# Column sums of the pruned attention gathered in 32 partitions of one column group instead of 4 x 8 rows in four

## The reference, cut to what matters

```
scores = softmax(einsum('bhqd,bhkd->bhqk', q, k) / sqrt(8))   # B=8, H=16, 128 x 128
col_sum = sum(scores, axis=2)                                 # over the queries: (B, H, 128)
_, idx = top_k(col_sum, int(128 * 0.9))                       # keeps 115, drops 13
mask = 1 at idx, 0 elsewhere
out = einsum('bhqk,bhkd->bhqd', scores * mask[:, :, None, :], v)
```

## Time and profile before

| | |
|---|---|
| median of 3 runs | 852.5 us (851.77 to 853.15) |
| the profiled execution's own time | 851.77 us |
| its span in the trace | 850.1 us |
| PE busy over the span | 730.0 us (86%) |
| mean granted clock of PE | 0.911 of full |
| pruned attention, first scores to last output | about 546.6 to 616.3 us |

### The profile page before, as it was taken

One profiled execution on the slowest core, in us unless ns is written; L12 is line 12 of the kernel. 1 busy time (PEld: TensorE's weight loads), 2 busy tenths in 40 slices (PEclk: granted clock), 3 DMA queues, 4 the chain that ended last, 5 costly groups with the idle time before them and its releaser, 6 DMA issues. The chain is left out here.

```text
span 850.1 us, 14512 instructions
## 1 busy us (share of the span) xinstructions
PE 730.0 (86%) x4910; PEld 610.7 (72%) x4910; DVE 557.7 (66%) x1478; ACT 415.5 (49%) x1279; POOL 374.2 (44%) x375
## 2 busy tenths in 40 slices
PE   5984899998999999986559999699769999994755
PEld 3653699997899998875557888466558888883754
DVE  6897664346799989874546677668645566655535
ACT  3891343443455555442135777389424466652221
POOL 6753212203566643533123776556431488872001
PEclk9798799999899999997879999869869999997678
DMA  7000010110000000000003444000100323100000
GB/s 268 2 1 25 13 50 27 49 49 1 1 1 2 7 2 1 2 1 0 7 19 128 138 134 156 2 1 3 38 26 10 108 84 111 52 12 0 1 1 25
DMA packets 14276, 33.11 MB, mean 39 GB/s; under 512 B 1744, under 2 KB 5864, under 8 KB 13952
## 3 DMA queue, kind: packets, MB, share of 16 engines
q1 hardware_dynamic: 14208, 32.26, 11.3%
HBM read 31.63 MB, written 0.62 MB: 38 GB/s over the span
## 5 line engine op out<-in xcount | busy, mean ns | idle before, releaser
L1205 PE MATMUL banks<-input_hi,weights_in_lo 128*128 128x512 f32 x296 | 125.9, 426 | 27.0 <-PEq L1482 14.1
L1205 PE MATMUL banks<-input_lo,weights_in_hi 128*128 128x512 f32 x296 | 120.9, 408 | 0.0
L1205 PE MATMUL banks<-input_hi,weights_in_hi 128*128 128x512 f32 x296 | 120.2, 406 | 0.0
L1205 PEld LDWEIGHTS banks<-weights_out,hidden 128*128 128x128 f32 x864 | 100.5, 192 | 3.1 <-DVE hidden L2232 1.0
L1205 PE MATMUL banks<-weights_out,hidden 128*128 128x128 f32 x864 | 101.3, 275 | 0.7 <-ACT att_feat L1124 0.7
L985 ACT ACTIVATE probabilities<-banks,neg_max 128x128 f32<-128x128 f32 x256 | 90.7, 425 | 14.2 <-DVE neg_max L1877 14.1
L1071 ACT ACTIVATE hidden<-banks,cols 128x512 f32<-128x512 f32 x80 | 54.2, 688 | 78.9 <-ACTq L1069 78.9
L697 POOL TENSOR_TENSOR rstd<-var_eps,neg_half 128x4 f32<-128x4 f32 x24 | 25.1, 1044 | 151.5 <-POOLq L696 139.9
L1205 PEld LDWEIGHTS banks<-input_hi,weights_in_lo 128*128 128x128 f32 x296 | 58.8, 199 | 41.3 <-issue 29.4
L807 POOL TENSOR_TENSOR hidden<-hidden,scratch 128x512 f32<-128x512 f32 x48 | 62.1, 1293 | 19.2 <-ACT hidden L1090 16.7
L1205 PEld LDWEIGHTS banks<-input_hi,weights_in_hi 128*128 128x128 f32 x296 | 58.8, 198 | 13.5
(11 more groups left out here) (272 smaller groups left out, 1759.9 us busy)
## 6 DMA issues: line engine op xcount, KB each, us to landing
scratch<-cw_rows SPq DMA_DIRECT2D x19, 512.0 KB, 3.8
weights_out<-w_in SPq DMA_DIRECT2D x17, 256.0 KB, 2.7
weights_in<-w_in SPq DMA_DIRECT2D x8, 512.0 KB, 3.6
weights_in<-w_in SPq DMA_DIRECT2D x9, 256.0 KB, 3.0
weights_in<-w_in SPq DMA_DIRECT2D x16, 128.0 KB, 2.2
weights_out<-w_in SPq DMA_DIRECT2D x16, 128.0 KB, 2.2
wq<-w1q_in SPq DMA_DIRECT2D x1, 1024.0 KB, 4.9
wo<-w1o_in SPq DMA_DIRECT2D x1, 1024.0 KB, 7.0
```

What stands on the lines that cost most here:

```text
L1205: return pe.matmul(o, l, rh, start=start, stop=stop, **kw)
```

## The change

The eight one-column windows of a unit become eight 32-column blocks of their own, 128 x 32 each, with the inverse sum of head i in column 8 * (n % 4) + i of block i. All eight matmuls of a unit now write the same 32 partitions (0 to 31), where row 8 * (n % 4) + i is head i of unit n. What follows works on 32 partitions: ranking, mask, and the transpose of the mask (moving operand 32 columns of the identity instead of 128, output 128 x 32 instead of 128 x 128). `keep_values` reads the turned mask as 32 adjacent columns. `r_spread` keeps its size and place.

```
-        r_spread = scratch[:, 8:10, :].rearrange("p a t -> p (a t)")
+        r_spread = scratch[:, 8:10, :].rearrange("p a (u h m) -> p (a u) h m", h=8, m=2 * H)
-        ranked = sb("ranked", [P, P + 8])
-        top = sb("top", [P, 2, 8])
-        kept = sb("kept", [P, P])
+        ranked = sb("ranked", [2 * H, P + 8])
+        top = sb("top", [2 * H, 2, 8])
+        kept = sb("kept", [2 * H, P])
         def own_inverse(n):
-            at = 7 + 256 * (n % 4)
-            return r_spread[:, at:at + 7 * 32 + 1:32]
-
-        def inverse_column(n, i):
-            at = 7 + 256 * (n % 4) + 32 * i - (2 * (n % 4) + i // 4)
-            return r_spread[:, at:at + 32]
+            flat = r_spread[:, n % 4, :, :].rearrange("p h m -> p (h m)")
+            at = 8 * (n % 4)
+            return flat[:, at:at + 7 * (2 * H + 1) + 1:2 * H + 1]
                     for i in range(8):
-                        own = slice(32 * (i % 4), 32 * (i % 4) + 32)
-                        m = mm(bank[4 + n // 4 % 2][own, 0:P], inverse_column(n, i),
+                        m = mm(bank[4 + n // 4 % 2][0:2 * H, 0:P], r_spread[:, n % 4, i, :],
                                prob[:, n // 2 % 2, 8 * (n % 2) + i, :],
-                               start=(n % 4 == 0 and i < 4), stop=(n % 4 == 3 and i >= 4))
+                               start=(n % 4 == 0 and i == 0), stop=(n % 4 == 3 and i == 7))
-                    pe.transpose(bank[4 + n // 4 % 2][:, P:2 * P], kept[:, :], ident[:, :])\
+                    pe.transpose(bank[4 + n // 4 % 2][:, P:P + 2 * H], kept[:, :], ident[0:2 * H, 0:2 * H])\
-                    dve.tensor_scalar(ranked[:, 0:P], sums[:, P - 1::-1][:, 0:P], -1.0, None,
+                    dve.tensor_scalar(ranked[:, 0:P], sums[0:2 * H, P - 1::-1][:, 0:P], -1.0, None,
-                    kept_at = bank[4 + n // 4 % 2][:, P:2 * P].rearrange("p (j m) -> p m j", j=4)[:, 0:8, :]
-                    four = "p b (g j) c -> p (b g) j c"
+                    kept_at = bank[4 + n // 4 % 2][:, P:P + 2 * H]
-                    dve.tensor_tensor(v_kept[:, :, :, :].rearrange(four, j=4), v_wide[:, :, :, :].rearrange(four, j=4),
-                                      kept_at[:, :, :, None].broadcast_to([P, 8, 4, 32]),
+                    dve.tensor_tensor(v_kept[:, :, :, :].rearrange("p b h c -> p (b h) c"),
+                                      v_wide[:, :, :, :].rearrange("p b h c -> p (b h) c"),
+                                      kept_at[:, :, None].broadcast_to([P, 2 * H, 32]),
                                       ALU.mult).then_inc(v_kept_ready, 1)
```

## The result

The changed kernel takes 867.14 us (median of 4 runs, 865.85 to 867.96), the kernel before beside it 852.65 (851.77 to 853.15): a ratio of 1.0170, with a 95% interval of 1.0152 to 1.0187. It is slower by 14.5 us; 867.5 was forecast, with a range of 862 to 891. The profiled execution has a span of 864.2 us against 850.1.

What follows compares the result with a forecast made beforehand. PE was taken to bound the stage's half-clock stretch and ACT the full-clock one, with PE the bound after the change. The profiled 851.8 us, +15.8 for longer sums and -0.1 for the other edits gave 867.5, range 862 to 891.

Steps and rivals of the forecast that it cites:

- The price of a group: Column sums: sixteen instructions queue in group 0 at 107 ns, 1.86 us for 0.58; +1.28 us a unit, +2.56 at half clock.
- Both bounds: Column sums, each unit: +0 if narrow weights alone are fast (chance 0.03), +3.0 us if weight loads no longer hide (0.04).
- The estimate from the page: Column sums: four groups gain 3.2 rather than 4, so a unit loses 1.17 us, the stage some 1.5 us less.
- The change of the bound: Plain step at full clock: PE takes 3.78 us, over ACT's 3.31, so PE becomes the bound and ACT waits.
- two variants: Whole stage: two half-clock steps end the last sums at 624.2, +17.5 us; one ends them at 620.9, +14.2.
- the middle: Whole stage: +15.8 us, taken between +17.5 for two half-clock steps and +14.2 for one.
- the cases in which sums in one group don't bring the clock back or let it fall: PE clock: low until first kept values, +36 us, 888, chance 0.24; falling after each batch, some +50, 902, chance 0.12.
- The sentence that weighed these cases: Against the clock falling after kept values: full-clock rows show 2.0 us of wide work in 3.3 and no fall.
- The edits at nothing: Mask transpose, ranking on 32 partitions, `keep_values`, strided inverse sums: all told -0.1 to -0.8 us, taken as -0.1.
- up to 2 us either way: Chain after the last sums: where exactly the clock falls again is worth up to 2 us, slower or faster.

Runs made afterwards that it cites:

- the first experiment: The changed kernel with matmul i of a unit writing group i % 4 again, ranking, mask and its transpose still on 32 partitions: 851.09 us, ratio to before 0.9994.
- the second experiment: The kernel before with only all eight matmuls of a unit writing group 0, ranking on 128 partitions and wide mask transpose kept: 865.47 us, ratio 1.0172.
- the last experiment: The changed kernel with 14 identity transposes before its first scores and 12 before the scores of unit 2: 863.77 us, ratio to the kernel before 1.0175.

## Why the prediction was right

**The price of a group.** Forecast +1.28 us a unit at full clock and +2.56 at half; measured 1.87 - 0.58 = 1.29 and 3.55 - 1.01 = 2.54. It came from two unlike rows: 64 instructions that go round four groups, and eight transposes in one. Both bounds fall, +0 (which would have needed 0.65 us for the sixteen) and +3.0. One argument was circular, though: the 107 ns "that a transpose needs" is four times the 27 and stands in no row, where transposes take 99 or 128 ns.

The estimate from the page "TensorE: Matmul & The Clock Gate" of the Trainium skill, Part 3, which gives 2.38 times for three column groups at 512 columns a matmul (here 128), was +1.17, less than the 1.29 measured. But it was taken on 1.71 us, without the 0.15 of entry and exit. Of the whole row four groups give 1.87 / 0.58 = 3.2 times and three 1.87 / 0.78 = 2.4, which is what the page and the estimate from it say; 3.2 times of 1.87 us is a loss of 1.29 as well. The full factor of four is in the pitch alone (107 ns against 27), so the prediction set aside a figure that these runs agree with.

**The change of the bound.** Forecast a plain step of 3.78 bound by PE; measured 3.79, with PE at 14.00 of 14.00. One detail was off: ACT's gaps do not stand before its exponentials but before its copies of the transposes (6.0 us of 42, waiting for PE at L1274). PE is the cause either way.

**The sum.** The forecast had two variants, one or two long steps at half clock, and took the middle, +15.8. The trace has the variant with one: a single step with its sums at 3.55 us, the clock back by 559.3. From the same start that variant gives 552.28 + 69.1 = 621.4, and the last sums end at 621.2. So the better account was +14.2; the middle missed the 14.5 of the medians by 1.3 us. That 867.5 still stands only 0.4 from 867.14 is in part luck: the change was put 1.2 too high, and the kernel before, at 852.65 in these runs, had been put 0.9 too low.

**The clock.** I gave 0.36 to the cases in which sums in one group don't bring the clock back or let it fall. They failed: the clock was back at the end of a stretch in which PE did almost nothing but those sums (555.76 to 559.31), and PEclk is 1.00 from 566 to 612. The sentence that weighed these cases counted 2.0 us of wide work in each 3.31; by the earlier trace rows a plain step has 1.02 + 0.58 = 1.60, and some 2.2 only with the kept values spread over four steps. The rule of the Trainium skill (page "TensorE: Matmul & The Clock Gate", Part 1), that activity releases the throttle, gave the right sign and the right variant. What the 14 us of the earlier trace rows at half clock lacked remains open: those steps had scores on two 32-row groups for 1.58 of 4.49 us, and no run here varies that. What the traces do show is an order: with four groups three sums ran at half clock (the kernel before and the first experiment), with three or two groups two, with one group one (the changed kernel and the second experiment). So the clock came back sooner where a unit's sums were longer; why is not shown.

**The edits at nothing.** Ranking on 32 partitions: MAX8 0.29 for 0.30, the chain from the start of the ranking to `kept` 623.20 - 621.35 = 1.85 for 1.92. Mask transpose: 0.24 for 0.33, worth about 0.25 us over the stage by the second experiment. `keep_values` 1.22 for 1.22. The first experiment, with all of these in, has a ratio of 0.9994 (0.9968 to 1.0020).

**What I left out.** The last `kept` took 1.23 us longer, and the output product came back to full clock, -1.74. Neither was in the sum, beyond the "up to 2 us either way" for the clock. They nearly cancel, which is luck.

## What to carry to other kernels

Before you gather small outputs on fewer partitions, ask which column groups the matmuls run in. In this kernel sixteen instructions of 32 columns took 0.58 us in four groups and 1.87 in one, and the price of a layout is (instructions in the longest queue) x (pitch of one group), read from any row that goes round the groups. PE's rest beside the bound pays for a part of it only: over twelve units at full clock 0.20 us more a unit cost 1.2 us, 0.41 cost 2.4 and 1.29 cost 11.8. Where PE has short gaps around a dense stretch, matmuls whose results nobody reads can keep its clock up: they won 3.0 us (by the ratio) to 4.3 (in the medians) here.

## What the runs showed of the hardware that was not expected

- **Transposes keep the clock up.** In the two runs with fillers on the kernel before, 26 transposes of the identity, in gaps of 1.8 and 1.7 us, hold PEclk at 1.00 from 548 on, where the kernel before has 0.58 and then 0.50 in the same stretches of 4 us. The Trainium skill, page "TensorE: Matmul & The Clock Gate", Part 4 on PE-mode transpose, says that full clock doesn't engage for transposes, since they don't count as busy work in the same way; here they kept it from falling, so they do count. That transposes alone bring it back is not shown.
- **A DVE instruction ended only with POOL's.** The last `kept` is the same 128-element TENSOR_SCALAR as the three before it, which take 0.21 us. In the changed kernel it runs from 623.20 to 624.90, and POOL's TENSOR_TENSOR from 622.49 to 624.83; in the kernel before it took 0.47 us, to 609.22, and there a TENSOR_SCALAR of POOL ran to 609.15. In the one-group experiment it took 1.64 us, again in step with POOL, and in the last experiment 1.70. In every trace but that with two groups the last `kept` is longer than the others and ends 0.07 to 0.09 us after a POOL instruction, whether it had 0.3 or 1.6 us of that instruction ahead of it; with two groups it began 0.07 us before the end and took 0.21. A MATCH_REPLACE8 of DVE beside the same POOL instruction (622.90) took its usual 0.27.

```profile
606.37 2.78 POOL L765 TENSOR_SCALAR weights_in_hi<-weights_in 128x1024 fp32r<-128x1024 f32 x1
608.75 0.47 DVE L1947 TENSOR_SCALAR kept<-ranked 128x128 f32<-128x128 f32 x1
```

The Trainium skill, page "GPSIMD Engine Reference", section Specifications, says that POOL shares its SBUF interfaces with VectorE, and names the two kinds of VectorE instruction that contend with it; the ends agree with that. The change brought it about by timing alone: POOL splits the next weights right after the last inverse sums, and the ranking now starts 1.3 us later against it. No run took POOL's instruction away, so the cause is argued from how the ends line up and not tested.
